# Delta heads with raw keys and queries: norms as token columns, from squares against 64 columns of ones

## The reference

```python
q = qkvc[..., :KDIM]; kk = qkvc[..., KDIM:2 * KDIM]; v = ...      # after a 4-tap causal convolution and silu
q = _l2norm(q)                       # a / max(sqrt(sum(a * a)), 1e-12)
kk = _l2norm(kk)
beta = sigmoid(b_raw); decay = exp(-exp(A_log) * softplus(a_raw + dt_bias))

def step(state, inp):                # over the 256 tokens
    state = state * d_t
    Sk = einsum('bhi,bhij->bhj', k_t, state)
    delta = (v_t - Sk) * b_t
    state = state + einsum('bhi,bhj->bhij', k_t, delta)
    o = einsum('bhi,bhij->bhj', q_t, state)

y = o * silu(z)
y = y * rsqrt(mean(y * y) + 1e-06) * norm_w
out = einsum('btv,ov->bto', y, W_out)
```

## Time and profile before

| what | value |
|---|---|
| median of 3 runs | 1953.5 us (1953.16 to 1955.55) |
| profiled execution, its own time | 1959.84 us |
| its span, first to last instruction | 1957.8 us |
| mean granted TensorE clock in it | 0.969 of full speed |
| TensorE, VectorE, ScalarE, GpSimd busy | 89%, 78%, 63%, 32% of the span |
| heads 1 to 14, one after another | 80.4 us a head on the mean (736.63 to 1861.95 us) |

### The profile page before, as it was taken

The page is one execution under the profiler, slowest core; times in us unless marked ns, Lnnn a source line. Parts: engine busy times, 40 slices in busy tenths (PEclk is TensorE's granted clock), DMA queues, the critical chain, the costliest instruction groups (busy, mean ns, idle before and its releaser), DMA issues.

```text
span 1957.8 us, 33489 instructions
## 1 busy us (share of the span) xinstructions
PE 1751.0 (89%) x12824; PEld 1303.0 (67%) x12824; DVE 1523.7 (78%) x2421; ACT 1226.5 (63%) x2155; POOL 635.2 (32%) x442
## 2 busy tenths in 40 slices
PE   7899999999989879988988999888998899988976
PEld 5676676767656556766766667666776666766765
DVE  7888888888774787888878878788787887877853
ACT  3343535344445567778777777778777786777762
POOL 2213222222230536145153250532614416144140
PEclk9999999999999889999999999999999999999988
DMA  3010111101032001101111011010110101101000
GB/s 132 32 63 31 62 43 49 62 31 62 1 99 67 17 1 40 48 23 34 39 39 33 23 33 50 28 33 23 34 55 23 33 23 33 55 23 33 7 2 22
DMA packets 51445, 75.37 MB, mean 39 GB/s; under 512 B 3393, under 2 KB 41793, under 8 KB 51185
## 3 DMA queue, kind: packets, MB, share of 16 engines
q1 hardware_dynamic: 51312, 73.55, 11.8%
HBM read 72.29 MB, written 1.25 MB: 38 GB/s over the span
## 4 chain that ended last, share of the span: by engine, by line
PE 37%; DVE 14%; ACT 13%; issue 5%; POOL 3%; POOLq 0%; ACTq 0%; DVEq 0%
PE bank L725 6%; PE bank L891 6%; PE bank L846 5%; DVE d_sil L1305 5%; POOL d_dec L1623 3%; PE bank L736 3%; DVE d_Rb L1371 2%; PE bank L784 2%; DVE d_X L1357 2%; DVE d_W L1379 2%; PE bank L794 2%; ACT d_V L1104 2%; PE bank L867 1%; PE bank L798 1%; PE bank L868 1%
## 5 line engine op out<-in xcount | busy, mean ns | idle before, releaser
L1305 DVE SCALAR_TENSOR_TENSOR d_sil<-d_pre,d_w,d_sil 128x1024 f32<-128x1024 f32 x192 | 298.1, 1553 | 5.9 <-ACT d_pre L1075 5.6
L1629 POOL TENSOR_TENSOR d_Rb<-d_V,d_ones 128x512 bf16<-128x512 f32 x32 | 51.6, 1631 | 705.6 <-ACT d_V L1104 705.6
L1357 DVE CAST_PREDICATED d_X<-tables_sb,bank 128x512 bf16<-128x512 int32 x192 | 134.4, 700 | 154.8 <-PE bank L784 152.3
L725 PE MATMUL bank<-xnT,d_w 128*128 128x512 f32 x480 | 246.9, 650 | 0.4
L189 PE MATMUL bank<-xnT,a_w 128*128 128x512 f32 x512 | 237.5, 598 | 0.0
L1139 ACT ACTIVATE d_T<-bank 128x512 bf16<-128x512 f32 x160 | 98.5, 616 | 115.4 <-PE bank L794 113.0
L846 PEld LDWEIGHTS bank<-d_W,d_N 128*128 128x128 f32 x1024 | 122.7, 193 | 35.0 <-DVE d_W L1379 22.4
L1623 POOL TENSOR_TENSOR d_dec<-d_dec,d_qk 128x384 f32<-128x384 f32 x128 | 134.3, 1075 | 35.0 <-DVE d_N L1338 35.0
L725 PEld LDWEIGHTS bank<-xnT,d_w 128*128 128x128 f32 x480 | 90.5, 204 | 79.9 <-issue 79.9
L189 PEld LDWEIGHTS bank<-xnT,a_w 128*128 128x128 f32 x512 | 91.0, 192 | 78.8 <-issue 78.8
L489 POOL TENSOR_TENSOR a_hidc<-a_hid,a_comb 128x512 f32<-128x512 f32 x32 | 44.5, 1392 | 295.0 <-DVE a_hid L336 295.0
(11 more groups left out here) (211 smaller groups left out, 4495.6 us busy)
## 6 DMA issues: line engine op xcount, KB each, us to landing
d_dec<-decay_scratch SPq DMA_DIRECT2D x32, 512.0 KB, 5.9
a_w<-w SPq DMA_DIRECT2D x16, 897.0 KB, 4.5
d_w<-w SPq DMA_DIRECT2D x16, 776.0 KB, 4.8
a_comb<-comb_scratch SPq DMA_DIRECT2D x16, 512.0 KB, 5.5
d_dec<-decay_scratch SPq DMA_DIRECT2D x32, 256.0 KB, 6.2
d_wo<-w SPq DMA_DIRECT2D x16, 256.0 KB, 3.1
f_w<-w SPq DMA_DIRECT2D x8, 256.0 KB, 4.0
tables_sb<-tables SPq DMA_DIRECT2D x1, 1056.0 KB, 9.2
```

Of the source, the lines that this page charges most:

```text
L725: last = pe.matmul(psum[bank][:, :], cols(slot, (c * KT + k) * P, P), xnT[:, k, h * HALF:(h + 1) * HALF], start=(k == 0), stop=(k == KT - 1))
L1305: dve.scalar_tensor_tensor(sil[c][:, :, :], pre[c % 2][:, :, tap:tap + S], cols(slot, OC + 4 * c + tap, 1), sil[c][:, :, :], ALU.mult, ALU ...
L1357: dve.copy_predicated(left(Xp[lv][:, v], lv), mask.unsqueeze(1).broadcast_to([P, 8, 64]).rearrange("p n (g w) -> p n g w", w=lv), psum[4 + ...
```

## The change

Keys and queries are left as silu gave them. With the raw k and q, the products are scaled afterwards: a row (token) of k k^T and of k q^T is divided by the squared norm of its key, V is multiplied by the norm of its key, and the norm of the query is put into the epsilon of y's root mean square, since y would only be scaled by it. All three are columns with one value a token, 8 columns for the 8 chunks. To get columns, TensorE takes the squares as the stationary side and 64 columns of ones as the moving side: 16 matmuls of 64 columns a head in place of 4 of 512.

What goes: the two wide `guard`s, `rnorm` (two Ln, two Exp of 1024 columns), `unit` (two of 1024 columns), the Ln and Exp of `scale_y`, GpSimd's rounding with ones. What comes: three small instructions in `guard` (8 columns), a Sqrt of 8 columns on ScalarE (`key_norm`), a Sqrt of y's mean squares (`root_y`) and its reciprocal on VectorE (`inverse_y`), each `d_kk` and each `d_qk` in two instructions with a column as scale, and on GpSimd for each value head a rounding of V times the norm (512) and V times the norm (1024). `project_z` for banks 0 and 1 no longer waits for `guard`.

```diff
             def project_z(slot, i, n):
-                pe.wait_ge(s["max_done"], i * 2 + n // 2 + 1)
+                if n < 2:
+                    pe.wait_ge(s["pre_done"], i * 8 + 5 + n)
+                    need(pe, s["acc_done"], (i - 2) * 4 + 3 + n)
+                elif n == 2:
+                    pe.wait_ge(s["kss_done"], i * 2 + 2)
+                else:
+                    pe.wait_ge(s["kss_done"], i * 2 + 1)
...
             def norms(i, c, h):
                 pe.wait_ge(s["sq_done"], i * 2 + c + 1)
-                pe.wait_ge(s["pre_done"], i * 8 + 4 + 2 * c + h + 1)
-                if c == 0:
-                    need(pe, s["acc_done"], (i - 2) * 4 + 2 + h + 1)
-                pe.matmul(psum[2 * c + h][:, :], onesf[:, :], nrm[c][:, h * HALF:(h + 1) * HALF],
-                          start=True, stop=True).then_inc(s["ssq_ready"], 1)
+                pe.wait_ge(s["pre_done"], i * 8 + 7 + c)
+                for t in range(4 * h, 4 * h + 4):
+                    last = pe.matmul(psum[2 + c][:, t * 64:(t + 1) * 64], sq[c][:, t * P:(t + 1) * P], onesf[:, 0:64],
+                                     start=True, stop=True)
+                if h:
+                    last.then_inc(s["ssq_ready"], 1)
...
-            def rnorm(i, c):
...
+            def key_norm(i):
+
+                act.wait_ge(s["kss_done"], i * 2 + 1)
+                need(act, s["vb_done"], i * 4)
+                act.activation(knorm[:, :], kss[:, :], ACT.Sqrt).then_inc(s["knorm_done"], 1)
...
-                act.activation(qk[b % 2][:, :, :], psum[5 + 2 * (b % 2)][:, 0:3 * P].rearrange("p (c t) -> p c t", c=3),
-                               ACT.Copy).then_inc(s["qk_done"], 1)
+                act.wait_ge(s["krec_done"], i + 1)
+                ps = psum[5 + 2 * (b % 2)][:, 0:3 * P].rearrange("p (c t) -> p c t", c=3)
+                act.activation(qk[b % 2][:, 0:2, :], ps[:, 0:2, :], ACT.Copy, scale=krec[:, 2 * b:2 * b + 1])
+                act.activation(qk[b % 2][:, 2, :], ps[:, 2, :], ACT.Copy,
+                               scale=krec[:, 2 * b + 1:2 * b + 2]).then_inc(s["qk_done"], 1)
...
-            def scale_y(i):
+            def root_y(i):
                 act.wait_ge(s["yssm_done"], i + 1)
-                act.activation(yss[:, :, :], yss[:, :, :], ACT.Ln).then_inc(s["ysqrt_ln"], 1)
-                act.wait_ge(s["ysqrt_ln"], i + 1)
-                act.activation(yrs[:, :, :], yss[:, :, :], ACT.Exp, scale=-0.5).then_inc(s["yrs_done"], 1)
+                act.activation(yss[:, :, :], yss[:, :, :], ACT.Sqrt).then_inc(s["ystd_done"], 1)
...
                 copy_qk(i, 3)
+                key_norm(i)
                 if not first:
-                    scale_y(i - 1)
+                    root_y(i - 1)
...
-            def guard(i, c, bank=0):
...
-            def unit(i, c):
...
+            def guard(slot, i):
+                dve.wait_ge(s["ssq_ready"], i * 2 + 2)
+                need(dve, s["knorm_done"], i)
+                dve.tensor_scalar(kss[:, :], psum[3][:, 0:HALF:64], 4e-24, None, ALU.max).then_inc(s["kss_done"], 1)
+                dve.tensor_scalar(qeps[slot][:, :], psum[2][:, 0:HALF:64], 4e-24, 16e-6, ALU.max, ALU.mult).then_inc(s["kss_done"], 1)
+                dve.wait_ge(s["kss_done"], i * 2 + 1)
+                need(dve, s["qk_done"], i * 4)
+                dve.reciprocal(krec[:, :], kss[:, :]).then_inc(s["krec_done"], 1)
...
-                dve.tensor_tensor(kk[b % 2][:, :, :], psum[4 + 2 * (b % 2)][:, 0:3 * P].rearrange("p (c t) -> p c t", c=3),
-                                  tabs["strict3"].rearrange("p (c t) -> p c t", c=3), ALU.mult).then_inc(s["kk_done"], 1)
+                dve.wait_ge(s["krec_done"], i + 1)
...
+                dve.scalar_tensor_tensor(kk[b % 2][:, 0:2, :], ps[:, 0:2, :], krec[:, 2 * b:2 * b + 1], strict[:, 0:2, :],
+                                         ALU.mult, ALU.mult)
+                dve.scalar_tensor_tensor(kk[b % 2][:, 2, :], ps[:, 2, :], krec[:, 2 * b + 1:2 * b + 2], strict[:, 2, :],
+                                         ALU.mult, ALU.mult).then_inc(s["kk_done"], 1)
...
+                if c == 0 and a == 0:
+                    dve.wait_ge(s["vb_done"], i * 4 + 2 * v + 2)
...
+            def inverse_y(i):
+                dve.wait_ge(s["ystd_done"], i + 1)
+                dve.reciprocal(yrs[:, :, :], yss[:, :, :]).then_inc(s["yrs_done"], 1)
...
                 fill[0][0].append(lambda: gate_z(i, 3))
+                if not first:
+                    fill[0][0].append(lambda: inverse_y(i - 1))
...
-                    mid[3], end[3] = [si(2)], [gd(0)]
-                    mid[4], end[4] = [si(3)], [gd(1)]
-                    mid[5] = [lambda: unit(ni, 0)]
+                    mid[3], end[3] = [si(2)], [lambda: guard(ns, ni)]
+                    mid[4] = [si(3)]
...
                     for v in range(2):
                         plain(v)
-                    unit(ni, 1)
...
-                for v in range(2):
-                    pool.wait_ge(s["v_done"], i * 4 + 2 * v + 2)
-                    pool.tensor_tensor(Rb[v][:, :, :], V[v][:, :, 0, :], onesf[:, :].unsqueeze(1).broadcast_to([P, B, P]),
-                                       ALU.mult).then_inc(s["vb_done"], 1)
...
                 decayed(i, slot, 3)
+                pool.wait_ge(s["knorm_done"], i + 1)
+                scale = knorm[:, :].rearrange("p (b c) -> p b c", c=2).unsqueeze(3).broadcast_to([P, B, 2, P])
+                for v in range(2):
+                    pool.wait_ge(s["v_done"], i * 4 + 2 * v + 2)
+                    pool.tensor_tensor(Rb[v][:, :, :], V[v][:, :, 0, :], scale[:, :, 0, :], ALU.mult).then_inc(s["vb_done"], 1)
+                    pool.wait_ge(s["vb_done"], i * 4 + 2 * v + 1)
+                    pool.tensor_tensor(V[v][:, :, :, :], V[v][:, :, :, :], scale, ALU.mult).then_inc(s["vb_done"], 1)
```

70 lines of the change are left out of this document (26 added, 44 removed).

## The result

| kernel | median | runs | against before, 95% interval |
|---|---|---|---|
| before | 1953.9 us (1953.16 to 1955.55) | 4 | |
| changed | 1939.4 us (1936.28 to 1941.97) | 4 | 0.992 (0.991 to 0.994) |
| forecast | 1932.5 us (1917 to 1948) | | |

The change is faster by 14.5 us, where 21 were forecast. The profiled execution of the changed kernel took 1936.28 us, with a span of 1934.4. The two profiled executions lie 23.4 us of span apart, more than the medians, since the one of before was 6 us slower than its median and the one of after 3 us faster.

A forecast was written before the change was run, and what follows sets the result against it. No engine was full, so savings counted only where an engine is waited for, plus TensorE's half clock. Terms of -9 (14 heads), -2 (last head and tail) and -10 (clock) took 1953.5 to 1932.5 us, range 1917 to 1948.

The forecast's parts named there:

- the -9 us forecast for the code of 14 heads: Sum of the per-head code terms, -0.65 us a head, over 14 heads.
- First term: Head start, ScalarE: one table load fewer, partly offset by split copies and added VectorE instructions; -0.6 us a head.
- Second term: Inverse's first level, VectorE: `inverse_y` adds 0.2 us, `d_gcol` shortens by 0.8, about half let through; -0.3 us a head.
- GpSimd in VectorE's way: Rival: GpSimd's longer work slows two more convolution steps on the chain; +0.6 us a head, 1941 us, chance 0.12.
- Third term: End of the inverse, ScalarE: the first tanh needs a table reload, exposed behind a wait; +1.3 us a head.
- the rival with the reload hidden: End of the inverse: the reload runs in ScalarE's idle time and only 0.3 us shows; 1918.5 us, chance 0.12.
- Fourth term: Solves, VectorE and TensorE: smaller guards, and the gate projection starts right behind `apply`; -1.05 us a head.
- Norms, 0: TensorE's norm matmuls: 32 records at 116 ns, 3.7 us, replace 3.4 to 4.3 us a head; no gain.
- GpSimd, 0: GpSimd's work ends 11 to 12 us later but before the solves, covered by 46.52 us of idle; no cost.
- Last head and tail, -2: Last head has no tanh (-0.6), and a load and activation in the tail become a reciprocal; -2 us together.
- The clock, -10: TensorE's idle gaps at the head start shrink, removing a bit more than half of 18.4 us of half clock; -10 us.
- Neither rival on the clock: Rivals: half clock stays as frequent, 1942.5 us, chance 0.20; new gap halves the clock in every head, 1960.5, chance 0.08.

The follow-up runs named there:

- e7: Changed kernel with early tanh table load, reciprocal of y's root ahead of the first level's mask, and 12 filling matmuls at the head start: 1907.3 us.
- e12: e7 with VectorE's copy of the decay columns also moved ahead of the first level's mask: 1907.7 us.
- e3: Changed kernel with the reciprocal of y's root moved on VectorE ahead of the first level's mask: 1932.4 us.
- e5: Changed kernel with GpSimd's scaling of y cut to 8 of 128 columns, output no longer the reference's: 1927.1 us.
- e6: e1 with 12 added matmuls filling TensorE's idle gap at the head start: 1926.9 us.
- e8: Changed kernel with the gate projections of banks 0 and 1 again waiting for the guard's first two instructions: 1939.7 us.
- e9: e8 with two 512-column VectorE instructions added ahead of the guard's small ones: 1958.4 us.
- e4: Kernel before the change with 24 filling matmuls in TensorE's idle gap at the head start: 1940.4 us.
- e2: Changed kernel with an extra one-column Tanh behind the root of y at the head start, moving the table load there: 1963.1 us.
- e11: e7 without its 12 filling matmuls: 1927.8 us.
- e1: Changed kernel with an extra one-column Tanh in level 5 of the inverse, so the table load runs early: 1929.8 us.

## Why the prediction was right or wrong

Direction and range held, and the total missed by 7 us. That it came so near is in part luck: of the -9 us forecast for the code of 14 heads nothing came (+0.6 in the profiled pair), and the clock, for which the forecast had only "a bit more than half", gave more than its share.

- **First term, -0.6: right**, -0.76. The last copy pair began 0.36 us later behind VectorE's first `d_kk` than the copy before (+0.3 forecast) and was 0.25 longer (+0.3). The load and the two tiny activations took 1.57 us to the copy of N where I had 1.75, and that is the difference.
- **Second term, -0.3: wrong**, +0.58 (1.82 less the 1.24 of the load). This is the step that failed: "Since GpSimd now waits for `inverse_y` (...), it is idle at that moment, and I expect the 0.16". It was, and `d_gcol` became short; but where that alone was added to e7 it was worth nothing, since TensorE's projection hides it (e12), though the chain of before passed through it. And I had not asked what GpSimd would meet 0.3 us later. e3 and e5 put that at 0.80 us a head. The rival "GpSimd in VectorE's way" had it with +0.6 and a chance of 0.12; it should have been in the sum. The Trainium skill's sentence on shared SBUF interfaces (GPSIMD Engine Reference, Specifications) was the hint to take it seriously. By these runs it holds unevenly: a step took 2.08 to 2.40 us beside the scaling of y or the mask, 1.40 beside the products with `d_qk` or a rounding of V, and 1.58 or 2.43 (changed kernel, e5) beside V times the norm with a rounding.
- **Third term, +1.3: right**, +1.24, and e6 gets 1.23 of it back; the rival with the reload hidden is out. Part of that flows into the contention with the mask unless GpSimd's work moves too.
- **Fourth term, -1.05: right**, -1.02, and the gate projection starts right behind `apply`, as forecast. The lost wait and the shorter guards are not two savings: the wait costs nothing behind a short guard (e8) and 0.94 us of TensorE behind a wide one (e9).
- **Norms, 0: right** for their own time. 8 records of 64 columns take 1.00 to 1.06 us, near the 8 x 116 ns that I had taken; with 8 columns they take 0.96 to 1.01. The section of the Trainium skill that the prediction quotes for N / 2.4 + 2.5 ns (TensorE: Matmul & The Clock Gate, Back-to-back issue gap) gives that for a matmul by itself, and says that with a weight load for each matmul both set the pace and the formula is too low at few columns; so the 1.8 us was not its forecast for this case. That the number of columns could matter through the clock, I had not seen.
- **GpSimd, 0: right by a hair.** I forecast all its work 11 to 12 us late and the mask done before the solves begin. It was 15.7 us late: behind the first `corner` the mask ended after 34.22 us and before after 18.54. That is 4.1 us into the solves (1260.88 against 1256.79) and 1.07 us ahead of the exponentials (1261.95). The two roundings and the two products took 8.7 us where I had 5.8 to 7.0, and its scaling of y and products with `d_qk` beside VectorE 10.6 in place of 7.6. e6 shows what lies beyond that point.
- **Last head and tail, -2:** the last head, from its first gate projection on, took 4.3 us less in the profiled executions. 2.1 of these are the last output projections, 9.22 us before and 7.14 after, at a higher clock; the other 2.2 are near the forecast and were not taken apart.
- **The clock, -10: wrong by a factor of 1.7** in the profiled pair. From the gate projection of head 1 to that of head 15 it is 1125.3 us before and 1108.6 after, or 14 x 78.96 + 19.9 and 14 x 79.00 + 2.6. That is -17.3 for the clock and +0.6 for the code. I took "a bit more than half" since two gaps of about 1 us remained; 8 of 11 heads escaped. Neither rival on the clock held: the stretches did not stay as frequent, and none began at the new gap.

The sum for the profiled pair: heads -16.7, last head and tail -4.3, head 0 and the feed-forward part +0.3, and 2.7 us that the changed kernel was ahead when layer 1 began (542.0 against 544.7 us), in a part that nobody touched. In the medians the clock's share must be smaller: 14.5 less 1.6 for code (+0.6 and -2.2) leaves an estimated 13 us. So nearly all of what the change gained is clock; without it, one ScalarE load fewer at the head start and the smaller guards were paid back by the reload and by GpSimd. e4 says the same from the other side: the filled gap alone gives the kernel before 15 us (1940.4 against 1955.3). Its heads are as long as those of both kernels (78.95, 78.96 and 79.00), so it is the shorter gap that most likely freed 8 heads in the changed kernel. A run of the changed kernel in which only this gap is long again was not made: e2 also takes the load out of the end of the inverse.

What stays open: why at equal gaps (1.04 and 0.93 us) the changed kernel and e5 have 3 heads with a stretch, e8 5, e3 6, e9 7, e11 8 and e1 14. Their heads differ in length and in what surrounds the gap. In e1 all 14 are alike, so it is not chance from head to head, but none of these runs varies the length of a head alone. The counts are of one execution each; the five of e3 spread over 7.8 us, by an estimate three stretches of 2.3 us.

## What to carry to other kernels

Before taking work off an engine, ask what the freed or moved engine will lie beside: here GpSimd's scaling moved onto two VectorE steps and took back 0.6 of the 1.8 us that the head start and the solves had gained, and one reciprocal put into idle time recovered it. A function change on ScalarE can cost its whole load, even where the engine idles just before: look which wait the load carries, and give it a tiny activation of the right function in an earlier idle place. Where TensorE idles a microsecond or two in each round of a loop, look at its granted clock first: here 24 unneeded matmuls in the gap were worth as much as the reworked algorithm, 12 in a smaller gap were worth 20.5 us, and matmuls made narrower cost 36 us.

## What the runs showed of the hardware

- Where its activation has two waits, the table load carries one of them: in `tanh_in` and `key_norm` the one that the code writes second. So at the end of the inverse it ran behind a wait of 1.00 us. With a single wait the load runs ahead of it (the last head of the kernel before: load at 1932.76, its activation at 1934.23 after 0.19 us of idle), and in e1 the early activation and its load have none (1246.12).
- One half-clock stretch costs a head 0.9 us in the changed kernel (79.00 to 79.89), 1.5 in the kernel before and 2.3 in e3 and e11. The stretch also shifts which VectorE steps fall beside which GpSimd instructions, which may be the difference; it wasn't isolated.
- Half clock at the head start went with TensorE's idle gap there: 2.24 us filled to 0.89 took it from 11 heads to 4 (e4), and 1.04 filled to 0.37 from 14 to none (e1 to e6).
- Matmuls of 8 columns in place of 64 took the same time, and the kernel 36 us more, with half clock in the solves.
- The same VectorE instruction of 16 columns took 0.11, 0.15, 0.86 and 1.03 us, by what GpSimd did beside it. The Trainium skill (SBUF — State Buffer, SBUF: two separate sides) says that for a VectorE instruction in a 2-port mode or with two SBUF inputs the later of the two engines is blocked until the other's whole instruction ends. The 0.86 to 1.03 would agree with that, since GpSimd's products there take 1.0 to 1.5 us each, but no run shows whether this instruction, with one input, is of that kind. A convolution step, which has two inputs and is only 0.12 us longer beside work without a break (1.40 against 1.28), doesn't show such a wait.
